# Attention: projections in halves behind pairs of heads, bursts of reciprocals, and the shift in the maxima's banks

## The reference

```python
H, D = 16, 32
q, k, v = moveaxis((x @ qkv_w + qkv_b).reshape(b, n, 3, H, D), 2, 0)
attn = softmax(einsum('bnhd,bmhd->bhnm', q, k) * D ** -0.5)
out = einsum('bhnm,bmhd->bnhd', attn, v).reshape(b, n, c) @ proj_w + proj_b
x = layernorm(x + out)
# then layernorm(x + cross_attention(ctx, x)), layernorm(x + experts(x))
```

## Time and profile before

| | us |
|---|---|
| timed runs, median of 3 | 3653.32 (3651.91 to 3653.96) |
| span of the profiled execution | 3644.6 |
| PE busy in it | 3423.0 |
| DVE busy | 2510.0 |
| POOL busy | 1995.2 |
| ACT busy | 1672.6 |

### The profile page before, as it was taken

The page is one execution under the profiler, slowest core; times in us unless marked ns, Lnnn a source line. Parts: engine busy times, 40 slices in busy tenths (PEclk is TensorE's granted clock), DMA queues, the critical chain, the costliest instruction groups (busy, mean ns, idle before and its releaser), DMA issues. The chain is left out here.

```text
span 3644.6 us, 50074 instructions
## 1 busy us (share of the span) xinstructions
PE 3423.0 (94%) x18021; PEld 2227.0 (61%) x18021; DVE 2510.0 (69%) x4512; ACT 1672.6 (46%) x3043; POOL 1995.2 (55%) x1008
## 2 busy tenths in 40 slices
PE   7999999999999999999999987999959899999996
PEld 5545455455455555455454435877739789988885
DVE  5777777777777777777777735889834765566667
ACT  2455555555555555555555553444312333233332
POOL 2688888888888888888898950011110101110112
PEclk9999999999999999999999998999969999999998
DMA  6322221321312312213120022132132333323332
GB/s 223 103 56 65 86 62 62 93 67 61 97 50 73 97 50 85 73 50 106 56 64 24 15 93 66 58 121 81 53 119 81 113 113 104 116 89 114 117 128 99
DMA packets 190278, 308.49 MB, mean 85 GB/s; under 512 B 25514, under 2 KB 72234, under 8 KB 190011
## 3 DMA queue, kind: packets, MB, share of 16 engines
q1 hardware_dynamic: 166970, 243.82, 21.8%
q0 software_dynamic: 14592, 44.32, 3.5%
q10 hardware_dynamic: 8448, 16.78, 1.3%
HBM read 195.66 MB, written 61.33 MB: 71 GB/s over the span
## 5 line engine op out<-in xcount | busy, mean ns | idle before, releaser
L511 DVE TENSOR_REDUCE sa_part_max<-sa_mx 128x1 f32<-128x512 f32 x2048 | 1282.4, 680 | 539.8 <-PE sa_mx L625 536.0
L466 ACT ACTIVATE sa_prob<-sa_sc 128x512 f32<-128x512 f32 x2010 | 1101.3, 595 | 803.7 <-PE sa_sc L692 764.4
L268 POOL TENSOR_TENSOR sa_quad_sum<-sa_quad_sum,sa_prob 128x1024 f32<-128x1024 f32 x500 | 1174.6, 2382 | 6.3 <-ACT sa_prob L466 6.3
L268 POOL TENSOR_TENSOR sa_quad_sum<-sa_prob 128x1024 f32<-128x1024 f32 x250 | 588.2, 2372 | 266.9 <-ACT sa_prob L466 266.9
L2055 PE MATMUL ex_h<-ex_xT,ex_w 128*128 128x384 f32 (+2 forms) x2688 | 463.9, 328 | 52.0 <-issue 24.4
L625 PE MATMUL sa_mx<-sa_k_even,sa_q_stack 96*128 96x512 f32 x1024 | 490.8, 483 | 17.2 <-DVE sa_part_max L511 7.5
L625 PE MATMUL sa_mx<-sa_k_odd,sa_q_stack 96*128 96x512 f32 x1024 | 476.6, 465 | 10.0 <-DVE sa_part_max L511 8.6
L2055 PEld LDWEIGHTS ex_h<-ex_xT,ex_w 128*128 128x128 f32 x2688 | 445.3, 194 | 64.8 <-issue 32.6
L692 PE MATMUL sa_sc<-sa_q_stack,sa_k_even 98*128 98x512 f32 x1024 | 427.1, 417 | 0.0
L2066 PE MATMUL ex_acc<-ex_w,ex_hT 128*128 128x512 f32 x1719 | 415.6, 392 | 1.9 <-DVE ex_hT L1994 1.6
L692 PE MATMUL sa_sc<-sa_q_stack,sa_k_odd 98*128 98x512 f32 x986 | 415.5, 423 | 1.6 <-ACT sa_prob L466 1.6
(11 more groups left out here) (229 smaller groups left out, 3776.8 us busy)
## 6 DMA issues: line engine op xcount, KB each, us to landing
ex_w_in<-in_L_ffn_w_dram SPq DMA_DIRECT2D x130, 512.0 KB, 4.1
sa_xT<-xT SPq DMA_DIRECT2D x57, 1024.0 KB, 5.1
sa_q_stack<-sa_hilo SPq DMA_DIRECT2D x372, 64.0 KB, 2.0
rows<-sa_empty SPq DMA_DIRECT2D x48, 257.0 KB, 3.7
ex_rows<-rows POOLq DMA_DIRECT2D x8, 1542.0 KB, 7.7
sa_k_odd<-sa_hilo SPq DMA_DIRECT2D x192, 64.0 KB, 2.0
ex_xg<-rows POOLq DMA_DIRECT2D x48, 256.0 KB
sa_k_even<-sa_hilo SPq DMA_DIRECT2D x168, 64.0 KB, 2.0
```

The source lines that it names most:

```text
L268: pool.tensor_tensor(quad_sum[:, i % 2, heads, :], so_far, prob[:, k, heads, :], ALU.add).then_inc(quad_ready, 1)
L466: act.activation(prob[:, kt % 4, j, :], score_bank(n)[:, :], ACT.Exp, scale=SCALE).then_inc(prob_ready, 1)
L511: dve.reduce_max(part_max[:, q, j, k:k + 1], mx[n % 3][:, :], AX_X).then_inc(max_read, 1)
```

## The change

The 12 whole parts per chunk become 24 halves (`project_half`). For q and k a half is one of four input blocks for 256 of the 512 columns, for v two of the four blocks for 128 columns. They stand behind pairs of heads, over all 16 steps (`HALVES_AT`). DVE empties `misc` at (4,1), (10,1) and, for the third job, at (0,1) of the next chunk, not at (4,1), (8,1), (12,1). The jobs' order changes a little (the v job of n = 2 goes to the end). The reciprocals are made two and two at (6,1) and (8,1), the division moves from quad 1 to quad 2, the store from step 10 to 13. The transposes of the shift no longer use `misc`: they take a turn in the three `mx` banks at (14,1), and DVE's cast stands at (14,1) too.

```diff
-    SUMS_AT, DENS_AT, DIVIDE_AT, STORE_AT = 0, 2, (1, 1), 10
-    INVERT_AT = ((3, 1), (3, 3), (4, 1), (4, 3))
+    SUMS_AT, DENS_AT, DIVIDE_AT, STORE_AT = 0, 2, (2, 1), 13
+    INVERT_AT = {(6, 1): (0, 1), (8, 1): (2, 3)}
+    SHIFT_AT = (14, 1)
...
-    PARTS_AT = ((0, 1, 2, 3), (4, 5, 6, 7), (8, 9, 10, 11))
+    HALVES_AT = (((0, 3), (1, 1), (1, 2), (1, 3), (2, 2), (2, 3), (3, 1), (3, 3)),
+                 ((4, 3), (5, 1), (5, 3), (6, 3), (7, 1), (7, 3), (8, 3), (9, 1)),
+                 ((10, 3), (11, 1), (11, 3), (12, 3), (13, 1), (13, 3), (14, 3), (15, 1)))
+    LEAVE_STEPS = (4, 10, T)
...
+    MAXIMA_TO_SHIFT = LEAD + SHIFT_AT[0] * PER_STEP + SHIFT_AT[1] + 1
+    SHIFT_PLACE = {min(g * NMAX + MAXIMA_TO_SHIFT, CHUNKS * NMAX) + g - 1: g for g in range(1, CHUNKS)}
...
+    def max_bank_free(engine, place):
+        old = place - len(mx)
+        if old in SHIFT_PLACE:
+            engine.wait_ge(shiftT_ready, SHIFT_PLACE[old] + 1)
+        elif old >= 0:
+            engine.wait_ge(max_read, old + 1 - sum(1 for other in SHIFT_PLACE if other < old))
...
-                    if i == 0 and kt == T - EARLY + 1 and g + 1 < CHUNKS:
+                    if (kt, i) == SHIFT_AT:
                         leave_shift(g + 1)
...
+        def project_half(i, half):
...
+            if job.what == "v":
+                t = half // 2
+                for k in (0, 1) if half % 2 == 0 else (2, 3):
+                    last = pe.matmul(misc[:, t * P:(t + 1) * P], xT[:, slot, k, t * P:(t + 1) * P], wkv[:, k, 1, :],
+                                     start=(k == 0), stop=(k == KC - 1))
+            else:
+                k = half % KC
+                cols = slice(half // KC * (BANK // 2), (half // KC + 1) * (BANK // 2))
+                weight = wq[:, k, :] if job.what == "q" else wkv[:, k, 0, :]
+                last = pe.matmul(misc[:, cols], weight, xT[:, slot, k, cols], start=(k == 0), stop=(k == KC - 1))
...
                     score(g, kt, i)
+                    if (kt, i) == SHIFT_AT and g + 1 < CHUNKS:
+                        transpose_shift(g + 1)
...
-                    if i == 2 and kt == T - EARLY and g + 1 < CHUNKS:
-                        transpose_shift(g + 1)
-                if (g, kt) in PART_AT:
-                    project_part(*PART_AT[g, kt])
+                    if (g, kt, i) in HALF_AT:
+                        project_half(*HALF_AT[g, kt, i])
```

More of the change, by code:

```diff
@@ L100, in self_attention @@
     LAST, LAST_DEN_AT = CHUNKS - 1, 11
-    SUMS_AT, DENS_AT, DIVIDE_AT, STORE_AT = 0, 2, (1, 1), 10
-    INVERT_AT = ((3, 1), (3, 3), (4, 1), (4, 3))
+    SUMS_AT, DENS_AT, DIVIDE_AT, STORE_AT = 0, 2, (2, 1), 13
+    INVERT_AT = {(6, 1): (0, 1), (8, 1): (2, 3)}
+    SHIFT_AT = (14, 1)
     Op = namedtuple("Op", "what n ahead c load")
     OPS = [Op("q", 2, 0, 0, 0), Op("k", 0, 1, 0, 1), Op("k", 1, 1, 0, 2),
-           Op("q", 3, 0, 1, 3), Op("k", 2, 1, 1, 4), Op("v", 2, 1, 1, 4),
-           Op("k", 3, 1, 2, 5), Op("q", 0, 1, 2, 6), Op("v", 3, 1, 2, 5),
-           Op("v", 0, 1, 3, 6), Op("q", 1, 1, 3, 7), Op("v", 1, 1, 3, 7)]
-    PARTS_AT = ((0, 1, 2, 3), (4, 5, 6, 7), (8, 9, 10, 11))
+           Op("q", 3, 0, 1, 3), Op("k", 2, 1, 1, 4), Op("k", 3, 1, 1, 5),
+           Op("q", 0, 1, 2, 6), Op("v", 3, 1, 2, 5), Op("v", 0, 1, 2, 6),
+           Op("q", 1, 1, 3, 7), Op("v", 1, 1, 3, 7), Op("v", 2, 1, 3, 8)]
+    HALVES_AT = (((0, 3), (1, 1), (1, 2), (1, 3), (2, 2), (2, 3), (3, 1), (3, 3)),
+                 ((4, 3), (5, 1), (5, 3), (6, 3), (7, 1), (7, 3), (8, 3), (9, 1)),
+                 ((10, 3), (11, 1), (11, 3), (12, 3), (13, 1), (13, 3), (14, 3), (15, 1)))
+    LEAVE_STEPS = (4, 10, T)
     LOADS = [(2, 0), (0, 1), (1, 1), (3, 0), (2, 1), (3, 1), (0, 1), (1, 1)]
@@ L125, in self_attention @@
     JOBS = [Job(0, what, n, None, None, None) for what, n in FIRST_OPS]
-    JOBS += [Job(u + o.ahead, o.what, o.n, u * NQ + o.c, u * len(LOADS) + o.load, PARTS_AT[i % 3])
+    JOBS += [Job(u + o.ahead, o.what, o.n, u * NQ + o.c, u * len(LOADS) + o.load, i % 3)
              for u in range(UNITS) for i, o in enumerate(OPS) if u + o.ahead < UNITS]
@@ L129, in self_attention @@
     VALUES = [i for i, job in enumerate(JOBS) if job.what == "v"]
-    PART_AT = {(job.chunk, kt): (i, part) for i, job in enumerate(JOBS) if job.place for part, kt in enumerate(job.place)}
-    LEAVE_AT = {(job.chunk, job.place[-1] + 1): i for i, job in enumerate(JOBS) if job.place}
+    HALF_AT = {(job.chunk, kt, j): (i, half) for i, job in enumerate(JOBS) if job.place is not None
+               for half, (kt, j) in enumerate(HALVES_AT[job.place])}
+    LEAVE_AT = {divmod(job.chunk * T + LEAVE_STEPS[job.place], T): i for i, job in enumerate(JOBS) if job.place is not None}
+    MAXIMA_TO_SHIFT = LEAD + SHIFT_AT[0] * PER_STEP + SHIFT_AT[1] + 1
+    SHIFT_PLACE = {min(g * NMAX + MAXIMA_TO_SHIFT, CHUNKS * NMAX) + g - 1: g for g in range(1, CHUNKS)}
+    PLACE_OF_SHIFT = {g: place for place, g in SHIFT_PLACE.items()}
     USERS = {}
@@ L148, in job_of, with place_of_max @@
         return next(i for i, job in enumerate(JOBS) if (job.unit, job.what, job.n) == (unit, what, n))
+    def place_of_max(n):
+        return n + max((n - MAXIMA_TO_SHIFT) // NMAX, 0)
     def left_psum(i):
@@ L510, in reduce_max @@
             q, j, k = m // (HG * KQ), m // KQ % HG, m % KQ
-            dve.reduce_max(part_max[:, q, j, k:k + 1], mx[n % 3][:, :], AX_X).then_inc(max_read, 1)
+            dve.reduce_max(part_max[:, q, j, k:k + 1], mx[place_of_max(n) % len(mx)][:, :], AX_X).then_inc(max_read, 1)
         def make_shift(g):
@@ L528, in leave_shift @@
             after(dve, shift_in, g * 16 * HG)
-            dve.tensor_copy(shiftT[:, :], misc[0:2 * HG, :]).then_inc(shiftT_ready, 1)
+            bank = mx[PLACE_OF_SHIFT[g] % len(mx)] if g > 0 else misc
+            dve.tensor_copy(shiftT[:, :], bank[0:2 * HG, :]).then_inc(shiftT_ready, 1)
         def invert(g, q):
@@ L565, in _ @@
                         leave_psum(LEAVE_AT[g, kt])
-                    if (kt, i) in INVERT_AT and g > 0:
-                        invert(g - 1, INVERT_AT.index((kt, i)))
+                    if g > 0:
+                        for q in INVERT_AT.get((kt, i), ()):
+                            invert(g - 1, q)
                 if kt == T - EARLY - 1 and g + 1 < CHUNKS:
@@ L591, in project_part @@
             job = JOBS[i]
-            first = job.place is None
-            bank = first_bank[i % 3] if first else misc
-            slot = job.n % 2 if first else job.load % 2
+            bank, slot = first_bank[i % 3], job.n % 2
             if part == 0:
                 if job.what == "q":
-                    pe.wait_ge(in_wq, (job.unit + 1) * 16 * KC)
+                    pe.wait_ge(in_wq, 16 * KC)
                 else:
[L599 to L609, removed]
+                    pe.wait_ge(in_wkv, 16 * (KC + 1))
+                pe.wait_ge(tr_read, (job.n + 1) * KC)
+                if i >= 3:
+                    pe.wait_ge(v_ready if JOBS[i - 3].what == "v" else hilo_ready, left_psum(i - 3))
             if job.what == "v":
@@ L618, in project_part @@
                 last.then_inc(proj_mm, 1)
+        def project_half(i, half):
+            job = JOBS[i]
+            slot = job.load % 2
+            if half == 0:
+                if job.what == "q":
+                    pe.wait_ge(in_wq, (job.unit + 1) * 16 * KC)
+                else:
+                    pe.wait_ge(in_wkv, (job.unit + 1) * 16 * (KC + 1))
+                after(pe, in_x[slot], 16 * loads_until(job.load))
+                if JOBS[i - 1].place is None:
+                    pe.wait_ge(shiftT_ready, 1)
+                else:
+                    pe.wait_ge(v_ready if JOBS[i - 1].what == "v" else hilo_ready, left_psum(i - 1))
+            if job.what == "v":
[3 more added lines that the diff above has]
+                                     start=(k == 0), stop=(k == KC - 1))
+            else:
+                k = half % KC
+                cols = slice(half // KC * (BANK // 2), (half // KC + 1) * (BANK // 2))
+                weight = wq[:, k, :] if job.what == "q" else wkv[:, k, 0, :]
+                last = pe.matmul(misc[:, cols], weight, xT[:, slot, k, cols], start=(k == 0), stop=(k == KC - 1))
+            if half == 2 * KC - 1:
+                last.then_inc(proj_mm, 1)
@@ L620, in max_pass @@
         def max_pass(n, m, g):
-            after(pe, max_read, n - 2)
+            place = place_of_max(n)
+            max_bank_free(pe, place)
             q, j, k = m // (HG * KQ), m // KQ % HG, m % KQ
             at = g % NQ * BANK + q * P
-            pe.matmul(mx[n % 3][:, :], q_stack[0:QK, j, at:at + P], k_stack[g // NQ % 2][0:QK, j, k * BANK:(k + 1) * BANK],
+            pe.matmul(mx[place % len(mx)][:, :], q_stack[0:QK, j, at:at + P], k_stack[g // NQ % 2][0:QK, j, k * BANK:(k + 1) * BANK],
@@ L626, in max_pass @@
                       start=True, stop=True).then_inc(max_mm, 1)
         def transpose_shift(g):
```

(5 more changed lines are left out.)

## The result

The changed kernel takes 3714.4 us (median of 4, 3708.0 to 3721.5) against 3653.0 (median of 4): ratio 1.0173, 95% interval 1.016 to 1.0185. It is slower by 61 us; 42 were forecast, in a range up to 3718.

A forecast was written before the change was run, and what follows sets the result against it. PE (94% busy) bounds the kernel, waiting in places for ACT and DVE. 27 chunks x 1.8 = +49, chunk 0 -3.5, last three -3: together +42 on 3653, so 3695 us, range 3670 to 3718.

The forecast's parts named there:

- A chunk with nothing in its way: Self-attention chunk without any new wait: 18.3 + 42.8 + 0.35 = 61.4 us, 3.5 less than before.
- the reciprocals' stall: PE's waits at steps 3 to 5 for DVE's reciprocals and evacuation: 1.3 us a chunk, to go.
- the better cover by halves: Times between PE's bursts, with projection halves behind every second pair of heads: 42.8 us a chunk, against 45.0 before.
- The three-half stretch: PE's time from one burst's end to the next burst, with three projection halves in it: 5.29 us.
- The pause: POOL's idle time after quad 2, needed by DVE's shift operation: next add ready at 15.0, quad ends 15.26, so gone.
- A: Rival, half the block: POOL still pauses after quad 2, DVE waits 1.5 us; chunk 63.0, 3595 us; chance 0.14.
- B: Rival, no block: DVE's shift operation runs between two POOL adds without waiting; 3545 us; chance 0.08.
- The price of the block: Cost per chunk when DVE's shift operation waits for POOL, PE stands and the clock slows: 4.97 + 0.4 us.
- the late chunk: Kernel before, shift operation at 2046.06 taking 3.92 us: burst 12 to burst 0 19.40 us, ordinarily 14.43.
- The stop: PE standing before head (13,3) while DVE waits for POOL and three maxima fill the banks: 3.3 us.
- Chunk 0: First self-attention chunk, without a divide, so its quad ends at 14.05, before the next add's 15.0: -3.5 us.
- The last three: Final chunks, already paying most of the wait before the change; less the reciprocals' stall: -3 us together.

The follow-up runs named there:

- the same digit in the kernel before: The kernel before with one edit, POOL's divide moved from quad 1 to quad 2: 3655.2 us, ratio 1.0009.

## Why the prediction was right, step by step

- A chunk with nothing in its way: forecast 61.4, measured 61.52. Its parts came out otherwise: the reciprocals' stall was worth 1.8, not 1.3 (the chunks of 63.28 and 61.52), the better cover by halves 1.7, not 2.2, so that the sum of 3.5 us owes something to luck. The 1.8 was measured in the changed kernel, where PE is faster; without the run that moves the reciprocals in the kernel before, it stays open how much of this is error and how much a stall that grew. The three-half stretch came out exact.
- The pause: asked for at 13.8, next add possible at 15.0, quad 15.26 long: 13.76, 14.96 and, in the run with ACT's shift, 15.29 (1066.76 to 1082.05). Shown by moving the divide, by moving the operation, and by the same digit in the kernel before. Rivals A and B, faster, did not occur; A's mechanism (a short wait for the quad's end) is what the digit does in the kernel before.
- DVE's operation, wait included: 3.8 forecast, 3.9 measured.
- The price of the block was the mis-sized term: 4.97 + 0.4 forecast, 5.87 measured. I took the late chunk's 4.97 whole. There the granted clock was 0.70 and 0.73 in two stretches of 3 us, which is 3.4 us at the 1.2 GHz level:

```profile
2053.00:2056.00 3.00, 3.00 (x22) 0.77 (x24) 1.37 (x3) 0.91 (x2) 3.00 (x2) 0.73 0.03 8
```

  In the changed kernel it is 3.4 us in only 9 of the chunks 2 to 27, and 6.8 us in the other 17. Counted from one shift to the next, the 9 take 66.62 us on average and the 17 take 67.90: over 61.52 that is 5.1 and 6.4, with 5.4 forecast. So the price was nearly right (0.3 too high) where the slow time was as long as in the late chunk, and what was missed is that it is mostly twice as long; why it differs from chunk to chunk stays open. The stop was rightly sized (3.42 us), the clock's part is 2.3.
- Chunk 0 was to gain 3.5 and gained 2.1 (100.03 to 164.47, 64.4 us, against 66.5). The last three were to gain 3 and lost 2.5. The divide's place is 2.8 of that (195.2 us, and 192.3 with the divide in quad 3); in both runs the last shift takes 9.3 us where it took 4.07 before, and why is not shown. With 0.6 more in each of 27 chunks (16 us) these terms are 23 us, where the medians are 19 above the forecast (61 against 42); the other 4 are within the spread of the runs.
- Two readings were off and changed little. 29 of the 32 shifts were cheap before, not 28: the third late one took 1.12, and the operation behind it 2.27. And the 8.7 us between the span and the timed median is not time around the program: in every run on record the time is 1.7 to 2.0 us above its own span, so the profiled execution of the kernel before was itself some 7 us faster than the median.
- The rule of the Trainium skill, "SBUF — State Buffer", section "SBUF: two separate sides", held: DVE's tensor_scalar of SBUF waited to the end of an instruction of POOL in nearly every chunk (3.9 us at the median). The section also names an operation with two SBUF inputs; the SCALAR_TENSOR_TENSOR behind it took 2.26 us in a late chunk of the run with the divide in quad 3:

```profile
1880.74 1.16 DVE L543 TENSOR_SCALAR sa_shift<-sa_top 128x16 fp32r<-128x16 f32 x1
1881.94 2.26 DVE L545 SCALAR_TENSOR_TENSOR sa_shift<-sa_top,sa_shift 128x16 fp32r<-128x16 f32 x1
```

By itself it takes 0.17 us, as in the first rows behind the result.

## What to carry to other kernels

An operation of 0.2 us can be cheap only because another engine happens to pause there; before moving that engine's work, or speeding up the pace between, find out whose pause it uses. Keep a DVE operation that waits like this one away from a POOL that runs nearly unbroken: give it to ACT, or keep the pause by putting POOL's extra work into another quad. A stop of PE can cost more than its length, for here the clock was slow after it (3.6 us of stop, 2.3 of slow clock).

## What the runs showed of the hardware

- DVE mostly did not get its turn between two of POOL's instructions when the second was ready: in 27 chunks of the changed kernel it waited through the end of one add and the whole of the next (3.6 to 4.0 us), and its last shift took 9.3 us, through several. It is not a rule without exception: at 1880.74 in the rows above the operation ended with one add (at 1881.90; the add ended at 1881.87) though the next followed at once, and it was the operation behind it that waited through that next one. The late chunks of the kernel before and of the run with the reciprocals back have the same.
- Around the end of a stop of 3.4 to 3.5 us the granted clock was at the 1.2 GHz level for 6.8 us in 17 chunks and for 3.4 us in 9, and 12 matmuls whose results nobody reads, put into the stop, kept it at 2.4 GHz.
